# A fused cross-attention and mixture-of-experts kernel: fewer filler matmuls ahead of the first transposes, the low parts of late weights on GpSimd instead of VectorE, and a reordered first unit

## The chip, the cores and the metric

The kernel runs on one core of one Trainium2 chip. The metric is the device time of one execution in microseconds (us), and the time of a kernel is the median of several executions. Before the change the runs gave 1058.31, 1061.67 and 1062.47 us.

## What is computed

For 8 batches of 512 tokens of width 256, in float32, with a context of 512 rows of width 128 for each batch (cut to what matters):

```python
def attention(q, kv):                      # 16 heads of width 64
    qh, kh, vh = split(q @ Wq), split(kv @ Wk), split(kv @ Wv)
    scores = einsum('bhnd,bhmd->bhnm', qh, kh) * 64 ** -0.5
    return join(softmax(scores) @ vh) @ Wo + bo

def experts(x):                            # 8 experts, top 2
    probs = softmax(x @ gate_w.T)
    comb = top-2 of probs, zero elsewhere
    return sum over e of (x @ expert_w[e].T + expert_b[e]) * comb[:, e]

x = x + tanh(g_xattn) * attention(layernorm(x), ctx)
x = x + tanh(g_ffn) * experts(layernorm(x))
```

## The kernel before, in words

Every float32 operand of a matmul is split in two: a high part, which ScalarE (ACT) makes by a copy in the rounded type, and a low part, which is the value minus the high part. Each product is then three matmuls: high by high, high by low, low by high. The low part of what lies in PSUM is made by VectorE (DVE). The low parts of the probabilities (L520) are made by GpSimd (POOL).

A batch is one iteration of 32 **units**: 8 pairs of heads by 4 tiles of 128 tokens. For one unit TensorE (PE) computes the scores of two heads (L1131) into one of two score banks, DVE takes their maximum (L826, `nmax`), ACT makes shifts of it (L655) and the exponential (L664) into one of two slots of `pf`, ACT copies that to half precision (L674, the high part of `p_s`), POOL subtracts (L520, the low part), the queue of SyncE (SP) transposes both parts by DMA, and PE multiplies them with the values six units later (L1147, `PV`). The exponential of unit n waits for the low part of unit n-2, since `pf` has two slots. Between the units each engine does **jobs**: the projections `q`, `k`, `v`, the transposes `xt`, `ot`, `x2t`, the output projection `wo`, the gate and the experts. Jobs are written to three PSUM banks in turn, so job n waits until job n-3 has been read out.

The order of the work is written out by hand: `PE_ORDER`, `ACT_ORDER`, `DVE_ORDER` and `POOL_ORDER` hold one string for each of the 32 rows (units) of an iteration, and each engine works them off in order. The iterations are FIRST (batch 0, without experts), six of LOOP, and LAST; EPI follows. Each iteration also does the experts of the batch before, and the last rows of an iteration do `NEXT_JOBS`, the transposes and first projections of the next batch. For batch 0 these run ahead of it, in the prologue: `xt` 0 and 1, `q` 0, `k` 0, and right behind the first scores `q` 1, `k` 1 and `bound`.

**The prologue.** The inputs and weights are loaded by SP's queue in the order x, context, the first quarter of `wq` (`early`, columns 0 to 255), `wk`, the rest of `wq` (`rest`, 768 columns by two halves of the contraction), `wv`, and small ones. `wq` is staged in `pf`, `wk` and `wv` in the first two slots of `pt_s`, so those must have been read before the first exponential, and before the first and second transposes. ACT makes the high parts (L557 to L592), DVE the low part of `early` (L857) and of `rest` (L871), POOL those of `wk` (L507) and `wv` (L509). PE meanwhile multiplies the identity with itself as a filler (`keep_busy`, L1156; float32, so that each call is two matmuls in the trace): 36 calls ahead of `xt` 0, 5 ahead of `q` 0, 2 ahead of `k` 0. DVE computes the largest `wv` (L865), the largest context value (L734) and their product (L737), which the job `bound` spreads to all partitions, and from which comes `v_mul`, the scale of the values (L770, L799). ACT waits at L595 and L596 for all low parts of `wq` and `wv`, ahead of the first exponential.

**The late weights.** `wo` and the experts' weights come in 12 pieces of 128x512 during FIRST: in the rows of `LATE_AT` (0 to 9, 13, 14) SP issues the load into a stage in `acc` or `xn` (L451), ACT makes the high part three rows later (`LATE_HI`, L650), DVE the low part four rows later (`LATE_LO`, L934). A piece is loaded into a slot of the stage only when that slot's last low part is done (`late_lo`).

```python
if kind == FIRST and n - LATE_LO in LATE_AT:
    h = LATE_AT.index(n - LATE_LO)
    dve.wait_ge(late_hi, h + 1)
    dve.tensor_tensor(late[h][2], late_raw(h), late[h][1].bitcast(F32), ALU.subtract)
```

## Time and profile before

| | before |
|---|---|
| median of 3 runs (range) | 1061.67 us (1058.31 to 1062.47) |
| profiled execution: its own time / span | 1055.02 / 1053.2 us |
| PE busy, matmul | 1007.7 us, 96% of the span |
| DVE busy | 859.2 us, 82% |
| ACT busy | 792.9 us, 75% |
| POOL busy | 610.4 us, 58% |
| DMA, mean | 144 GB/s |
| granted TensorE clock, mean | 0.994 |

The span is the time from the first to the last instruction of the profiled execution. The busy shares are averages over stages with different limits: a few microseconds of prologue, the FIRST iteration, in which PE has no experts to compute, the loop and the end. In the sections below "us" after a row's start is counted from the start of the span, and L numbers are lines of the kernel before.

### The profile page before, as it was taken

The numbers are of one execution on the slowest core, as the hardware profiler recorded it, in microseconds if no ns is written. First come the engines' busy times: TensorE is split into PE (matmuls) and PEld (weight loads), VectorE is DVE, ScalarE is ACT, GpSimd is POOL, SyncE is SP. The second block draws the span as 40 slices with busy tenths as digits, with TensorE's granted clock in tenths as the row PEclk, the third lists the DMA queues.
The fourth block names the chain that finished last, engine by engine and source line by source line (L and its number), as shares of the span: only waits on it lengthen the run. The fifth ranks groups of instructions, "written<-read, shape, count | busy, mean of one in ns | idle before, by whom it ended". The sixth has DMA issues, their size and how long they took to land.

```text
span 1053.2 us, 29369 instructions
## 1 busy us (share of the span) xinstructions
PE 1007.7 (96%) x10752; PEld 779.6 (74%) x10752; DVE 859.2 (82%) x1537; ACT 792.9 (75%) x1404; POOL 610.4 (58%) x359
## 2 busy tenths in 40 slices
PE   7788999999999999999899999999999999999998
PEld 6456777777777777777677787777777787777786
DVE  5898778977888788987689788897889888897737
ACT  4889999767987599866798579885798659975600
POOL 3566767645774467644576446754677446864500
PEclk9999999999999999999999999999999999999999
DMA  4899999977997699965999759977799759996630
GB/s 136 163 207 163 166 175 174 160 112 117 191 184 130 100 169 178 170 120 93 165 179 154 127 89 197 181 135 119 138 184 172 121 101 167 171 156 121 111 62 20
DMA packets 554305, 152.11 MB, mean 144 GB/s; under 512 B 541976, under 2 KB 551600, under 8 KB 554160
## 3 DMA queue, kind: packets, MB, share of 16 engines
q1 hardware_dynamic: 554160, 150.18, 84.0%
q8 instruction: 90, 1.47, 0.6%
q14 instruction: 55, 0.45, 0.2%
HBM read 11.70 MB, written 4.19 MB: 15 GB/s over the span
## 4 chain that ended last, share of the span: by engine, by line
PE 69%; DVE 13%; ACT 7%; issue 7%; DMA 2%; POOL 1%; SPq 0%; DVEq 0%; ACTq 0%; POOLq 0%
PE MB L1021 34%; PE ST L1131 15%; PE PV L1147 13%; DVE nmax L826 4%; PE MB L1033 3%; ACT pf L664 3%; DMA pt_s<-p_s 2%; DVE acc L789 2%; PE ST L1156 2%; ACT p_s L674 1%; POOL p_s L520 1%; DVE m L964 1%; PE MB L1097 1%; DVE ex_s L934 1%; DVE ot_s L815 1%
## 5 line engine op out<-in xcount | busy, mean ns | idle before, releaser
L520 POOL TENSOR_TENSOR p_s<-pf,p_s 128x1024 f16<-128x1024 f32 x256 | 549.7, 2148 | 343.0 <-ACT p_s L674 329.8
L826 DVE TENSOR_REDUCE nmax<-ST 128x2 f32<-128x1024 f32 x256 | 310.9, 1216 | 49.7 <-PE ST L1131 47.4
L664 ACT ACTIVATE pf<-ST,shifts 128x512 f32<-128x512 f32 x512 | 325.4, 693 | 3.9 <-POOL p_s L520 0.4
L674 ACT ACTIVATE p_s<-pf 128x1024 f16<-128x1024 f32 x256 | 272.8, 1066 | 5.6 <-DMA pt_s<-p_s 1.9
L1147 PEld LDWEIGHTS PV<-v_s,pt_s 128*128 128x128 f16 x6144 | 202.9, 98 | 85.1 <-issue 73.4
L1147 PE MATMUL PV<-v_s,pt_s 128*128 128x65 f16 x6144 | 231.6, 194 | 9.8 <-DVE o_n L842 9.3
L1021 PE MATMUL MB<-ex_s,x2t_s 128*128 128x512 f32 x708 | 190.6, 405 | 1.0 <-DVE QL L806 1.0
L789 DVE SCALAR_TENSOR_TENSOR acc<-MB,m,acc 128x256 f32<-128x256 f32 x236 | 113.6, 481 | 45.3 <-PE MB L1021 34.7
L1021 PEld LDWEIGHTS MB<-ex_s,x2t_s 128*128 128x128 f32 x708 | 125.8, 189 | 29.3 <-issue 2.9
L1131 PE MATMUL ST<-KH,QH 64*128 64x512 f32 x512 | 125.6, 487 | 22.8 <-ACT pf L664 17.2
L655 ACT ACTIVATE shifts<-nmax 128x2 f32<-128x2 f32 x256 | 53.5, 212 | 96.6 <-DVE nmax L826 91.1
L1021 PEld LDWEIGHTS MB<-wo_s,ot_s 128*128 128x128 f32 x768 | 99.2, 190 | 11.4 <-DVE ot_s L815 5.1
L1021 PE MATMUL MB<-wo_s,ot_s 128*128 128x256 f32 x768 | 105.0, 286 | 1.6 <-DVE ot_s L815 1.3
L1021 PE MATMUL MB<-xt_s,wq_s 128*128 128x512 f32 x384 | 104.1, 406 | 0.5 <-issue 0.5
L1131 PE MATMUL ST<-KL,QH 64*128 64x512 f32 x512 | 102.0, 393 | 0.0
L1131 PE MATMUL ST<-KH,QL 64*128 64x512 f32 x512 | 101.8, 393 | 0.0
L1131 PEld LDWEIGHTS ST<-KH,QH 64*128 64x128 f32 x512 | 48.2, 184 | 67.7 <-issue 31.7
L574 ACT ACTIVATE ot_s<-MB 128x512 fp32r<-128x512 f32 x64 | 38.6, 605 | 61.0 <-PE MB L1033 61.0
L1021 PEld LDWEIGHTS MB<-xt_s,wq_s 128*128 128x128 f32 x384 | 67.5, 189 | 13.1 <-issue 1.8
L842 DVE SCALAR_TENSOR_TENSOR o_n<-PV,o_mul,rden 128x256 f32<-128x256 f32 x128 | 62.0, 484 | 4.5
L1021 PE MATMUL MB<-wv_s,kv_s 128*128 128x512 f32 x192 | 57.1, 422 | 2.5 <-DVE QL L806 2.5
L818 DVE SCALAR_TENSOR_TENSOR v_s<-MB,v_mul,v_s 128x512 f16<-128x512 f32 x64 | 46.9, 744 | 13.1 <-ACT v_s L578 13.1
(129 smaller groups left out, 1091.2 us busy)
## 6 DMA issues: line engine op xcount, KB each, us to landing
pt_s<-p_s SPq DMA_TRANSPOSE x512, 3.4
xin<-x SPq DMA_DIRECT2D x7, 512.0 KB, 4.6
out<-acc SPq DMA_DIRECT2D x7, 512.0 KB, 3.5
kvin<-kv_t SPq DMA_DIRECT2D x8, 256.0 KB, 4.4
acc<-expert_t SPq DMA_DIRECT2D x6, 256.0 KB, 4.1
pf<-wq SPq DMA_DIRECT2D x1, 768.0 KB, 7.6
xin<-x SPq DMA_DIRECT2D x2, 256.0 KB, 3.0
pt_s<-wk SPq DMA_DIRECT2D x1, 512.0 KB, 6.1
```

The source lines that it names most:

```text
L520: pool.tensor_tensor(p_s[:, slot, 1, :, :], pf[:, u % 2, :, :], p_s[:, slot, 0, :, :], ALU.subtract).then_inc(p_lo, 1)
L574: last = act.activation(ot_s[:, 0, name[1] % GROUP, :], m[:, :], ACT.Copy)
L655: act.activation(shifts[:, u % 2, :], nmax[:, u % 2, :], ACT.Identity, bias=P_SHIFT, scale=SCALE)\
L664: last = act.activation(pf[:, u % 2, i, :], ST[u % 2][:, i, :], ACT.Exp, bias=shifts[:, u % 2, i:i + 1], scale=SCALE)
L674: act.activation(p_s[:, it.ring(p, u, P_SLOTS), 0, :, :], pf[:, u % 2, :, :], ACT.Copy).then_inc(p_hi, 1)
L789: last = dve.scalar_tensor_tensor(acc[:, t, :], m[:, DIM * i:DIM * (i + 1)], comb[:, t, 2 * e + i:2 * e + i + 1], acc[:, t, :], ALU.mult, ...
L818: last = dve.scalar_tensor_tensor(v_s[:, 1, t, g * HH:(g + 1) * HH, 0:HEAD], m[:, :].rearrange("p (h d) -> p h d", d=HEAD), v_mul[:, 0:1], ...
L826: dve.tensor_reduce(nmax[:, t % 2, :], ST[t % 2][:, :, :], AX.X, ALU.max, negate=True)\
L842: dve.scalar_tensor_tensor(dst, outs[:, :, 0:HEAD], o_mul[:, 0:1], rden[:, :].unsqueeze(2).broadcast_to([P, TT, HEAD]), ALU.mult, ALU.mult ...
L1021: last = pe.matmul(dst, s, m, start=(k == 0), stop=(k == n - 1))
L1131: last = pe.matmul(ST[t % 2][:, i, :], queries[r, s, tile(t)], keys[r, s, :], start=(n == 0), stop=(n == len(terms) - 1))
L1147: last = pe.matmul(PV[:, col:col + HEAD + 1], pt_s[:, slot, a, i, k, :], v_s[:, c, k, (2 * p + i) % HEADS, :], start=(k == 0 and n == 0), ...
```

## The change

1. `BUSY_PRO`: the filler calls ahead of the first transposes go from 36 to 15.
2. The low parts of the 12 late weights move from DVE (row n+4) to POOL (row n+3).
3. The low part of `rest` is made in two halves: DVE makes one, behind the job `k` 0 and ahead of the first maximum; POOL makes the other, between `wk` and `wv`. ACT waits for both halves and no longer for `wv`. SP waits for `wv`'s low part ahead of the transposes of unit 1, and PE ahead of `q` 2 for both halves.
4. `NEXT_JOBS`: `bound` comes ahead of `q` 1 and `k` 1. The list sets the order in the prologue; for the other iterations the jobs stand in `PE_ORDER`, which is unchanged. The low part of `eb` and the scaling of `bo_t` on DVE come behind the take of `k` 1.
5. In row 0 of FIRST ACT does the copy of unit 0 ahead of the high part of the first values.

```diff
--- before.py
+++ after.py
@@ -115,7 +115,7 @@
 LATE_AT = list(range(10)) + [13, 14]
 LATE_SLOT = [0, 1, 2, 3, 0, 1, 2, 3, 0, 1, 0, 1]
 LATE_IN_XN = 8
-LATE_HI, LATE_LO = 3, 4
+LATE_HI, LATE_LO = 3, 3
 
 
 def job_of(token):
@@ -127,7 +127,7 @@
 PLACED = [job_of(token) for row in PE_ORDER for token in row.split() if token not in ("scores", "values")]
 
 
-NEXT_JOBS = [("xt", 0), ("xt", 1), ("q", 0), ("k", 0), ("q", 1), ("k", 1), ("bound",)]
+NEXT_JOBS = [("xt", 0), ("xt", 1), ("q", 0), ("k", 0), ("bound",), ("q", 1), ("k", 1)]
 
 LATE_JOBS = [("ot", PAIRS - 2), ("ot", PAIRS - 1)] + [("wo", ROUNDS - 1, j) for j in range(MT)]
 SUMMED = [name for name in PLACED if name[0] in ("bias", "expert")]
@@ -143,7 +143,7 @@
 PRO_JOBS = 4
 NEXT_X2T = [name for name in LAST_JOBS if name[0] == "x2t"][0]
 BUSY_VALUES = 3
-BUSY_PRO = {("xt", 0): 36, ("q", 0): 5, ("k", 0): 2}
+BUSY_PRO = {("xt", 0): 15, ("q", 0): 5, ("k", 0): 2}
 BUSY_EPI = {("ot", PAIRS - 1): 3, ("wo", ROUNDS - 1, 0): 6, NEXT_X2T: 24, ("router",): 5, ("logits",): 3}
 
 JOBS = {PRO: NEXT_JOBS, EPI: LATE_JOBS + LAST_JOBS}
@@ -332,7 +332,7 @@
         wq_in, wq_rest_in, wk_in, wv_in = sem("wq_in"), sem("wq_rest_in"), sem("wk_in"), sem("wv_in")
         small_in = sem("small_in")
         late_in = [sem(f"late_in{n}") for n in range(4)]
-        w_hi, wq_lo, w_lo = sem("w_hi"), sem("wq_lo"), sem("w_lo")
+        w_hi, wq_lo, wq_rest_lo, w_lo = sem("w_hi"), sem("wq_lo"), sem("wq_rest_lo"), sem("w_lo")
         late_hi, late_lo = sem("late_hi"), sem("late_lo")
         const_pool, const_dve = sem("const_pool"), sem("const_dve")
         tanh_done = sem("tanh_done")
@@ -449,6 +449,8 @@
                     if LATE_SLOT[h] in LATE_SLOT[:h]:
                         sp.wait_ge(late_lo, h - LATE_SLOT[:h][::-1].index(LATE_SLOT[h]))
                     sp.dma_start(late_raw(h), late[h][0]).then_inc(late_in[LATE_SLOT[h]], 16)
+                if it.kind == FIRST and n == 1:
+                    sp.wait_ge(w_lo, 2)
                 turn_hi(it, *divmod(n, TT))
                 turn_lo(it, *divmod(n, TT))
                 if n == 9 and it.kind != LAST:
@@ -505,7 +507,9 @@
             pool.wait_ge(ln1_done, 1)
             pool.wait_ge(w_hi, 2)
             pool.tensor_tensor(wk_s[:, 1, :], stage_k, wk_s[:, 0, :].bitcast(F32), ALU.subtract).then_inc(w_lo, 1)
-            pool.wait_ge(w_hi, 3)
+            pool.wait_ge(w_hi, 4)
+            pool.tensor_tensor(wq_s[:, 1, 1, rest], stage_q[:, 1, rest], wq_s[:, 0, 1, rest].bitcast(F32),
+                               ALU.subtract).then_inc(wq_rest_lo, 1)
             pool.tensor_tensor(wv_s[:, 1, :], stage_v, wv_s[:, 0, :].bitcast(F32), ALU.subtract).then_inc(w_lo, 1)
             pool.wait_ge(w_hi, 5)
             pool.tensor_tensor(gt_s[:, 1, :, :], gt_f[:, :, :], gt_s[:, 0, :, :].bitcast(F32), ALU.subtract)\
@@ -547,6 +551,11 @@
                         power(it.b + 2, ln1_var, ln1_rstd, ln1_shift)
                     elif part == "context" and it.kind != LAST:
                         context_low(it)
+                if it.kind == FIRST and n - LATE_LO in LATE_AT:
+                    h = LATE_AT.index(n - LATE_LO)
+                    pool.wait_ge(late_hi, h + 1)
+                    pool.tensor_tensor(late[h][2], late_raw(h), late[h][1].bitcast(F32), ALU.subtract)\
+                        .then_inc(late_lo, 1)
 
             run(pool, row)
             power(BATCHES, ln2_var, ln2_rstd, ln2_shift)
@@ -593,7 +602,7 @@
                     act.activation(tg[:, :], gates[:, :], ACT.Tanh).then_inc(tanh_done, 1)
                 take_hi(pro, name)
             act.wait_ge(wq_lo, 2)
-            act.wait_ge(w_lo, 2)
+            act.wait_ge(wq_rest_lo, 1)
 
             def context_high(it):
                 act.wait_ge(kv_in, 16 * it.b + 32)
@@ -618,7 +627,10 @@
 
             def row(it, n):
                 b, kind = it.b, it.kind
-                for part in ACT_ORDER[n].split():
+                parts = ACT_ORDER[n].split()
+                if kind == FIRST and n == 0:
+                    parts.sort(key=lambda part: part == "hi")
+                for part in parts:
                     at = count.get(part, 0)
                     count[part] = at + 1
                     if part == "hi":
@@ -866,17 +878,17 @@
                        .then_inc(const_dve, 1)
                     dve.wait_ge(const_dve, 1)
                     bound(0)
-                if name == ("q", 1):
+                take(pro, name)
+                if name == ("k", 0):
                     dve.wait_ge(w_hi, 4)
-                    dve.tensor_tensor(wq_s[:, 1, :, rest], stage_q[:, :, rest], wq_s[:, 0, :, rest].bitcast(F32),
+                    dve.tensor_tensor(wq_s[:, 1, 0, rest], stage_q[:, 0, rest], wq_s[:, 0, 0, rest].bitcast(F32),
                                       ALU.subtract).then_inc(wq_lo, 1)
-                if name == ("bound",):
+                if name == ("k", 1):
                     dve.wait_ge(w_hi, 6)
                     dve.tensor_tensor(eb_s[32:32 + EXPERTS, :], eb[32:32 + EXPERTS, :],
                                       eb_s[32:32 + EXPERTS, :].bitcast(F32), ALU.subtract).then_inc(const_dve, 1)
                     dve.wait_ge(tanh_done, 1)
                     dve.tensor_scalar(bo_t[:, :], bo_t[:, :], tg[:, 0:1], None, ALU.mult).then_inc(const_dve, 1)
-                take(pro, name)
 
             for name in JOBS[PRO][:PRO_JOBS]:
                 take_first(name)
@@ -928,11 +940,6 @@
                         moments(ln2_step, b, ln2_var)
                     elif part.startswith("route") and kind != FIRST:
                         route(it, int(part[-1]))
-                if kind == FIRST and n - LATE_LO in LATE_AT:
-                    h = LATE_AT.index(n - LATE_LO)
-                    dve.wait_ge(late_hi, h + 1)
-                    dve.tensor_tensor(late[h][2], late_raw(h), late[h][1].bitcast(F32), ALU.subtract)\
-                       .then_inc(late_lo, 1)
 
             GATE_STEPS = 18
             ROUTE_PARTS = 7
@@ -1053,6 +1060,7 @@
                     pe.wait_ge(kv_lo, it.b + 2)
                 elif kind == "q" and it.kind == FIRST and name[1] == 2:
                     pe.wait_ge(wq_lo, 2)
+                    pe.wait_ge(wq_rest_lo, 1)
                 elif kind == "v" and it.kind == FIRST:
                     pe.wait_ge(w_lo, 2)
                 elif kind == "bound":
```

How DVE's order moves at the end of the prologue. Before, from the context's maximum to the second score maximum:

```order
L734 TENSOR_REDUCE kmax<-kvin 128x1
L737 TENSOR_TENSOR kmax<-kmax,wv_max 128x1
L806 TENSOR_TENSOR QL<-MB,QH 128x512
L806 TENSOR_TENSOR KL<-MB,KH 128x512
L826 TENSOR_REDUCE nmax<-ST 128x2
L871 TENSOR_TENSOR wq_s<-pf,wq_s 128x2x768
L806 TENSOR_TENSOR QL<-MB,QH 128x512
L806 TENSOR_TENSOR KL<-MB,KH 128x512
L875 TENSOR_TENSOR eb_s<-o_n,eb_s 8x256
L878 TENSOR_SCALAR bo_t<-bo_t,tg 128x256
L770 TENSOR_SCALAR v_div<-MB 128x1
L799 RECIPROCAL v_mul<-v_div 128x1
```

The same place on DVE in the changed kernel (its own line numbers):

```order
L746 TENSOR_REDUCE kmax<-kvin 128x1
L749 TENSOR_TENSOR kmax<-kmax,wv_max 128x1
L818 TENSOR_TENSOR QL<-MB,QH 128x512
L818 TENSOR_TENSOR KL<-MB,KH 128x512
L884 TENSOR_TENSOR wq_s<-pf,wq_s 128x768
L838 TENSOR_REDUCE nmax<-ST 128x2
L782 TENSOR_SCALAR v_div<-MB 128x1
L811 RECIPROCAL v_mul<-v_div 128x1
L818 TENSOR_TENSOR QL<-MB,QH 128x512
L818 TENSOR_TENSOR KL<-MB,KH 128x512
L888 TENSOR_TENSOR eb_s<-o_n,eb_s 8x256
L891 TENSOR_SCALAR bo_t<-bo_t,tg 128x256
```

The subtraction for `wq` is half as long and stands ahead of the first maximum, and `v_div` and `v_mul` stand behind it, ahead of `q` 1 and `k` 1.

POOL from the prologue on, before (`p_s` is the low part of a unit's probabilities):

```order
L507 TENSOR_TENSOR wk_s<-pt_s,wk_s 128x1024
L509 TENSOR_TENSOR wv_s<-pt_s,wv_s 128x1024
L511 TENSOR_TENSOR gt_s<-o_n,gt_s 128x16
L520 TENSOR_TENSOR p_s<-pf,p_s 128x1024 x10
L534 TENSOR_TENSOR x<-xin,bo_t 128x1024
```

The same place on POOL in the changed kernel:

```order
L509 TENSOR_TENSOR wk_s<-pt_s,wk_s 128x1024
L511 TENSOR_TENSOR wq_s<-pf,wq_s 128x768
L513 TENSOR_TENSOR wv_s<-pt_s,wv_s 128x1024
L515 TENSOR_TENSOR gt_s<-o_n,gt_s 128x16
L524 TENSOR_TENSOR p_s<-pf,p_s 128x1024 x4
L557 TENSOR_TENSOR wo_s<-acc,wo_s 128x512
L524 TENSOR_TENSOR p_s<-pf,p_s 128x1024
L557 TENSOR_TENSOR wo_s<-acc,wo_s 128x512
L524 TENSOR_TENSOR p_s<-pf,p_s 128x1024
L557 TENSOR_TENSOR wo_s<-xn,wo_s 128x512
```

The half of `wq` stands ahead of `wv`, and from unit 3 on a piece of a late weight stands behind each unit's low part, twelve in all (units 3 to 12, 16 and 17).

## Rows read from the trace of the kernel before

**Rows 1.** Engines' busy time by stretch: times, engines (instructions), clock, DMA share, GB/s

```profile
210.00:330.00 120.00, 119.18 (x1310) 91.93 (x1309) 101.21 (x186) 97.32 (x172) 75.17 (x42) 1.00 0.90 149
...
38.90:94.92 56.02, 44.65 (x535) 32.64 (x534) 49.48 (x67) 48.76 (x90) 36.76 (x20) 0.97 1.08 203
...
94.92:150.00 55.08, 51.45 (x636) 40.07 (x637) 43.59 (x64) 52.30 (x93) 38.55 (x19) 0.97 1.01 161
```

**Rows 2.** The chain of waits from 0 to 45 us: start, us, what

```profile
3.04 9.97 PE ST L1156 x72
...
15.50 1.63 PE MB L1021 x6
...
21.92 1.68 DVE wq_s L871
...
23.86 1.27 ACT pf L664 x2
...
26.48 3.70 PE MB L1021 x9
...
31.26 1.24 DVE nmax L826
```

**Rows 3.** Timeline of the prologue: start, us, engine, instruction [idle before]

```profile
7.19 1.38 DVE L728 TENSOR_SCALAR xn<-xin,mv,rstd 128x256 f32<-128x256 f32 x4
8.90 1.06 ACT L561 ACTIVATE wk_s<-pt_s 128x1024 fp32r<-128x1024 f32 x1 [0.92 <-DMA pt_s<-wk]
...
13.48 1.09 ACT L570 ACTIVATE xt_s<-MB 128x512 fp32r<-128x512 f32 x2 [3.53 <-PE MB L1033]
14.11 1.29 DVE L808 TENSOR_TENSOR xt_s<-MB,xt_s 128x512 fp32r<-128x512 f32 x2 [4.81 <-ACT xt_s L570]
14.46 1.06 ACT L587 ACTIVATE wv_s<-pt_s 128x1024 fp32r<-128x1024 f32 x1
15.59 2.41 POOL L509 TENSOR_TENSOR wv_s<-pt_s,wv_s 128x1024 fp32r<-128x1024 f32 x1 [3.14 <-ACT wv_s L587]
17.28 0.58 ACT L568 ACTIVATE QH<-MB 128x512 fp32r<-128x512 f32 x1
18.94 0.69 DVE L806 TENSOR_TENSOR KL<-MB,KH 128x512 fp32r<-128x512 f32 x1 [0.32 <-ACT KH L568]
...
28.12 0.69 ACT L578 ACTIVATE v_s<-MB,v_mul 128x512 f16<-128x512 f32 x1 [2.02 <-DVE v_mul L799]
```

**Rows 4.** The load of `wv`: its issue in the timeline

```profile
3.73 0.47 SPq L413 DMA_DIRECT2D pt_s<-wv  x1
```

**Rows 5.** The DMA view to 25 us: size, median us from issue to landing

```profile
pt_s<-wv SPq DMA_DIRECT2D x1, 512.0 KB, 8.3
```

**Rows 6.** PE alone by stretches of 1 us: busy (matmuls begun), granted clock, DMA

```profile
6.00:7.00 1.00, 1.00 (x8) 1.00 0.97 366
7.00:8.00 1.00, 1.00 (x11) 1.00 0.99 392
...
27.00:28.00 1.00, 1.00 (x4) 0.52 0.00 0
```

**Rows 7.** Timeline: a low part of probabilities on POOL, a late weight on DVE

```profile
39.11 2.14 POOL L520 TENSOR_TENSOR p_s<-pf,p_s 128x1024 f16<-128x1024 f32 x1 [0.45 <-ACT p_s L674]
...
39.59 2.21 DVE L934 TENSOR_TENSOR wo_s<-acc,wo_s 128x512 fp32r<-128x512 f32 x1 [0.78 <-ACT wo_s L650]
```

**Rows 8.** Line L934: ns min/median/max, first and last start us

```profile
L934 DVE TENSOR_TENSOR ex_s<-acc,ex_s x6: 674/1453/2583, 54.6 to 93.3; 128x512 fp32r<-128x512 f32 x6
...
L934 DVE TENSOR_TENSOR wo_s<-xn,wo_s x2: 1622/1658/1694, 47.9 to 51.2; 128x512 fp32r<-128x512 f32 x2
```

**Rows 9.** Waits from 38.90 to 94.92: us in total, times, longest

```profile
POOL p_s L520 <- ACT p_s L674: 18.7, 12, 2.9
...
ACT shifts L655 <- DVE nmax L826: 7.0, 5, 1.9
```

**Rows 10.** Groups on POOL over the span: count, busy us, mean ns, idle before

```profile
L520 POOL TENSOR_TENSOR p_s<-pf,p_s 128x1024 f16<-128x1024 f32 x256 | 549.7, 2148 | 343.0 <-ACT p_s L674 329.8 <-DMA pt_s<-p_s 11.2
...
L525 POOL TENSOR_TENSOR kv_s<-kvin,kv_s 128x512 fp32r<-128x512 f32 x7 | 9.1, 1297 | 32.7 <-ACT kv_s L601 32.7
```

## The prediction

> **What bounds the kernel now.** I read the busy time by stretch first. In the loop PE is busy 119.18 of 120 us [rows 1]: nothing the change touches runs there, and every batch takes as long as its matmuls. Two stretches are left. Up to about 31 us the chain of waits goes in single file over PE, ACT and DVE. From 38.90 to 94.92 us (units 4 to 18 of FIRST, in which all twelve late weights are split) no engine is full: PE 44.65, DVE 49.48, ACT 48.76, POOL 36.76 of 56.02 us [rows 1]. From there to 150 us ACT is busy 52.30 of 55.08 us [rows 1], the change touches nothing, and the stretch should only move. So what is gained or lost by 95 us is handed on to the end, since PE then only begins its full loop earlier or later.
>
> In the chain of the prologue the reader is to see three long pieces [rows 2]: fillers, 9.97 us; the low part of `wq`, 1.68 us between the first maximum and the first exponential; and nine matmuls of the values, 3.70 us, at the granted clock of about half [rows 6]. The first exponential starts at 23.86, the maximum of unit 2 at 31.26 [rows 2]; at that maximum I measure the prologue's gain.
>
> **The start, step by step.** The fillers run from 3.04 to 13.01. Their rate rises from 8 to 11 a microsecond at 7 us [rows 6]. 30 matmuls instead of 72: 26 are begun by 7 us, by the rows before 7 us and the 8 in the last, and four at the faster rate end at 7.4. The last tile is normalised at 7.19 + 1.38 = 8.57 [rows 3], so the eight transposes now wait for DVE and end near 9.3; the fillers cost nothing any more. ACT is at the high part of `wk` until 8.90 + 1.06 = 9.96, since its load lands late [rows 3]. The high parts of `xt` run from 9.9 to 11.0 where they ran from 13.48, and the low parts end at 11.85 instead of 15.40 [rows 3]. Next in line is the load of `wv`: issued at 3.73 [rows 4] and 8.3 us to landing [rows 5], it is there at 12.0 to 12.5. So ACT starts `wv` at 12.3 and not at 14.46 [rows 3]: of the 3.5 us that the transposes come earlier only 2.2 are left. All that stands between `wv` and the high part of `q` 0 on ACT takes 17.28 - 14.46 = 2.82 us [rows 3] and stays, so that part starts at 15.1. The low part of `k` 0 ended at 19.63 [rows 3] and now ends at 17.0, if `k` 0 follows as closely: **2.6 us** gained at the first scores.
>
> Then the moved subtraction. DVE starts its half of `rest` at 17.0. It reads two tensors from SBUF, and a look at rows 7 shows what that means: at 39.59 a late weight started on DVE while POOL worked from 39.11 to 41.25, and it ended at 41.80, 0.55 us after POOL, though alone it takes 0.67 [rows 8]. POOL has the high parts of `wq` at 14.8 here, does its half in 768/1024 of 2.41 us [rows 3], 1.8 us, and then `wv`, from 16.6 to 19.0. So DVE's half waits and ends near 19.8 (0.55 + 0.27 for the 256 further columns), 1.75 us after the scores are ready. The first maximum follows, and the first exponential at 21.2 instead of 23.86: still 2.6 us. The old 1.68 us behind the maximum are gone, and a wait of about the same size stands ahead of it. From below the cost of this half is 0.9 us alone, hidden behind the first scores, and from above 2.4 us, all of `wv`; I take 1.75, as the order of starts gives it.
>
> Behind it `bound` is taken 0.4 us after the first maximum, so `v_mul` no longer stands behind `q` 1, `k` 1, `eb` and `bo_t`, and ACT's wait of 2.02 us for it [rows 3] is gone. The copy of unit 0 stands ahead of the values and does not need `v_mul` at all. PE can do the first values' job while ACT is at the exponential; the second and third still need the banks of `q` 1 and `k` 1. I work out the low parts of `q` 1 and `k` 1 by 24.3, the maximum of unit 1 at 25.1 to 26.3, the low part of the first values, and the maximum of unit 2 at 27 instead of 31.26: **4.0 us** gained (2.6 kept, 1.4 more as the nine value matmuls are no longer one block behind a wait). `eb` and `bo_t` are only moved and cost what they did. The new wait of SP for `wv` (19.0) costs nothing: the transposes of unit 1 come ten microseconds later. The wait of PE ahead of `q` 2 is long met.
>
> **The late weights.** DVE gets rid of twelve subtractions. Alone one takes 0.674 us, the median of six is 1.453 [rows 8], since most start under POOL; together about 18 us. What this holds up is ACT: it waited 7.0 us for maxima [rows 9]. POOL gets twelve of the shape of its context step, 1.297 us each [rows 10]: 15.6 us. Its waits for ACT were 18.7 us there [rows 9], so there is room, but only just: 36.76 + 15.6 = 52.4 us of work in what were 56.02 [rows 1]. ACT's own work, 48.8 us, allows a gain of 7.2; POOL's allows 3.6, and that only if it never waits. A unit and a late weight take 2.15 + 1.30 = 3.45 us on POOL [rows 10], against some 48.76 / 15 = 3.25 us a unit on ACT. POOL becomes the tightest engine in units 3 to 12. Its bubbles (at the start of the stretch, and where a copy comes late) I put at 1.3 us, a tenth of a microsecond for each piece: **2.3 us** gained. Bounds: 7.0 gained, ACT's waits [rows 9], if POOL's order lets ACT run freely, and 8.6 lost, as the first rival has it; I stay near POOL's own floor of 3.6, since its work is counted from rows and only its bubbles are a guess.
>
> The Trainium skill speaks against this part: "GPSIMD Engine Reference", section Engine selection, puts elementwise work with two inputs on VectorE, since GpSimd is about twice as slow. The rows agree on the size, 1.297 against 0.674. By that rule alone the twelve would cost 12 x 0.62 = 7.5 us and the sum would be 3.5 us slower, near 1065; the median of 1.453 and the free time of POOL are why I go by the rows.
>
> Sum: 4.0 + 2.3 = 6.3 us. The profiled execution took 1055.02 us (span 1053.2 and 1.8 around it) and would come to 1048.7. The median of the runs lies 6.6 us above it, so for the changed kernel's median I forecast 1061.67 - 6.3 = 1055.4 us. About 0.5%, 5.3 us, is what a measurement of this kernel can tell from no change.
>
> **The rivals.**
>
> *POOL becomes the bound and it is slower.* A late weight sits between two low parts. If each delays the next low part, the exponential two units later and the scores behind it, 12 x 1.30 = 15.6 us stand on the path, of which the 7.0 us of ACT's waits come back: 8.6 lost, less 4.0 of the start, 4.6 us slower, 1066.3. It decides where more than 11 of the 15.6 us are not hidden. For it: several of POOL's waits were short (0.45 us at 39.11 [rows 7]). Against: they sum to 18.7 us.
>
> *The clock falls at the start.* PE now idles from 10 to 11.9 and from 15 to 17 us, where fillers kept it busy. Between 24 and 26.5 it idled once before, and the clock was 0.52 afterwards [rows 6]. Six matmuls took 1.63 us at the full clock, nine would take 2.45 and took 3.70 at the half [rows 2]: 0.14 us each. Some 15 on the path: 2 us of the gain go, 1057.4. The Trainium skill, "TensorE: Matmul & The Clock Gate", section PE-mode transpose, adds that transposes do not count as busy for the clock. By it the clock would fall already behind the shorter fillers, with the same price.
>
> *More than forecast.* DVE's half is not held up, because POOL starts `wv` later, and POOL keeps up: 1.75 and some 3 us more, a gain of 11, 1050.7.
>
> *The gain is not handed on.* The stretch after 95 us, where DMA was busy at a share of 1.01 [rows 1], takes back what was gained; near 1061.
>
> **How the numbers follow.** Forecast (a gain of 3 to 9 us) 0.56, more 0.13, clock 0.13, not handed on 0.08, POOL as the bound 0.10. Range: 1050.5 to 1062.0, from the good rival to no gain; it leaves out the slower one and half of what is beyond either end. Faster by over 0.5%: 0.13 and 0.42 of the forecast's 0.56, 0.55. Slower by over 0.5%: 0.06 of the last. Within: 0.39.
>
> **What would show it.** First transposes at about 8.7; ACT's `wv` at 12.3 behind its DMA; DVE's half of `wq` drawn out to about 2.8 us, ending 0.8 behind POOL's `wv`; first exponential at 21, maximum of unit 2 near 27. In the middle stretch ACT's waits for maxima gone, waits for POOL's low parts in their place, and POOL above 90% busy in units 3 to 12. Wrong it is if the unit-2 maximum comes as forecast and the end doesn't, or if POOL's low parts of units 4 to 18 take more than the 56 us they did.

## The result, and the profile after

The changed kernel takes 1050.38 us (median of 5 runs, 1048.92 to 1050.84) against 1059.11 (5 runs, 1056.07 to 1062.47) of the kernel before. The ratio is 0.991, with a 95% interval from 0.989 to 0.9929. That is faster by 8.7 us at the medians. The forecast was 6.3 us: the direction was right, the size too small, and 1050.38 lies just outside the range, whose lower end was 1050.5.

The two profiled executions differ by less: 1055.02 before, 1048.92 after, 6.1 us. The sum had been made against the first of them, so the total of the forecast fits the traces. Its parts don't: one was too large, one too small, and a third (what is given back later) stood at nothing. That they sum to nearly the right number is luck.

The page of the changed kernel, its first lines:

```profile
span 1047.1 us, 29286 instructions
...
PE 1002.5 (96%) x10710; PEld 773.6 (74%) x10710; DVE 846.3 (81%) x1525; ACT 792.6 (76%) x1404; POOL 627.3 (60%) x372
```

PE has 42 matmul instructions fewer (the fillers), DVE lost 13 us of work, and POOL took on 17.

The timeline of the start of the changed kernel (start, us, engine, instruction, idle time before it), answering to [rows 3]:

```profile
3.03 5.22 PE L1164 MATMUL ST<-ident 128*128 128x128 f32 x30 [3.03 <-POOL ident L492]
...
9.47 1.06 ACT L570 ACTIVATE wk_s<-pt_s 128x1024 fp32r<-128x1024 f32 x1 [0.76 <-DMA pt_s<-wk]
...
12.71 1.06 ACT L596 ACTIVATE wv_s<-pt_s 128x1024 fp32r<-128x1024 f32 x1 [1.20 <-DMA pt_s<-wv]
...
15.22 1.80 POOL L511 TENSOR_TENSOR wq_s<-pf,wq_s 128x768 fp32r<-128x768 f32 x1 [2.17 <-ACT wq_s L598]
15.55 0.57 ACT L577 ACTIVATE QH<-MB 128x512 fp32r<-128x512 f32 x1
16.98 2.38 POOL L513 TENSOR_TENSOR wv_s<-pt_s,wv_s 128x1024 fp32r<-128x1024 f32 x1
17.36 2.81 DVE L884 TENSOR_TENSOR wq_s<-pf,wq_s 128x768 fp32r<-128x768 f32 x1
...
24.93 2.33 POOL L524 TENSOR_TENSOR p_s<-pf,p_s 128x1024 f16<-128x1024 f32 x1 [4.68 <-ACT p_s L686]
...
25.29 2.12 DVE L891 TENSOR_SCALAR bo_t<-bo_t,tg 128x256 f32<-128x256 f32 x1
27.33 1.21 DVE L838 TENSOR_REDUCE nmax<-ST 128x2 f32<-128x1024 f32 x1
...
29.12 1.21 DVE L838 TENSOR_REDUCE nmax<-ST 128x2 f32<-128x1024 f32 x1
```

Read it from the top. The fillers end at 8.25, the load of `wv` is what ACT waits for (1.20 us), and its high part of `q` 0 starts at 15.55 instead of 17.28. DVE's half of `wq` (17.36) starts just behind POOL's `wv` (16.98) and takes 2.81 us; it ends at 20.17, 0.8 behind POOL. The surprise is `bo_t`: the scaling of 256 columns takes 2.12 us, where it took 0.35 before. It starts at 25.29, in the middle of POOL's first low part (24.93 to 27.26), and ends 0.15 us behind it. In the kernel before it ran while POOL was idle:

```profile
27.41 0.35 DVE L878 TENSOR_SCALAR bo_t<-bo_t,tg 128x256 f32<-128x256 f32 x1
```

The maximum of unit 1 stands behind it, at 27.33 and not at 25.1 as forecast, and that of unit 2 starts at 29.12: 2.1 us earlier than before [rows 2], not 4.0.

By the maximum of unit 4 (36.11 before, 35.12 after) only 1.0 of the 2.1 are left. PE alone in the changed kernel from 31 to 37 us:

```profile
31.00:37.00 6.00, 4.79 (x17) 0.50 0.47 91
```

The granted clock is at the lower level (1.2 of 2.4 GHz) from 30.3 to 37.2 us. A pair of score matmuls takes 0.80 us there instead of 0.50, and the maxima of units 3 and 4 wait for these matmuls. Before, this place ran at the full clock. The low clock comes with the loss but isn't shown to be all of it: in another execution of the kernel before (e5 below) units 2 to 4 took 6.0 us, as here, at the full clock up to 35.8 us.

The middle, in the stretches of time of [rows 1], and in that from the maximum of unit 5 to that of unit 19; columns as there:

```profile
38.90:94.92 56.02, 47.85 (x597) 34.86 (x596) 39.27 (x64) 53.33 (x97) 52.04 (x33) 1.00 1.09 200
...
94.92:150.00 55.08, 51.38 (x649) 39.45 (x647) 41.81 (x62) 52.79 (x94) 39.82 (x19) 1.00 1.11 172
```

```profile
38.57:87.69 49.12, 41.67 (x503) 30.20 (x503) 32.77 (x54) 46.69 (x86) 46.91 (x30) 1.00 1.09 201
```

DVE went from 49.48 us to 39.27 in the same stretch of time [rows 1], in which it gets further now, and POOL from 36.76 to 52.04. From the maximum of unit 5 to that of unit 19 both ACT (46.69 of 49.12 us) and POOL (46.91, 95%) are full. Two neighbours on POOL there, and the waits from 38.57 to 87.69 us (in total, times, longest):

```profile
52.15 2.15 POOL L524 TENSOR_TENSOR p_s<-pf,p_s 128x1024 f16<-128x1024 f32 x1
54.24 1.29 POOL L557 TENSOR_TENSOR ex_s<-acc,ex_s 128x512 fp32r<-128x512 f32 x1
```

```profile
POOL p_s L524 <- ACT p_s L686: 1.8, 3, 1.2
```

```profile
ACT pf L676 <- POOL p_s L524: 1.0, 1, 1.0
...
ACT shifts L667 <- DVE nmax L838: 0.7, 1, 0.7
```

The late weight takes 1.29 us, as forecast. POOL's waits for ACT fell from 18.7 us [rows 9] to 1.8, ACT's for maxima from 7.0 to 0.7, and ACT waited only once for POOL, 1.0 us. The maximum of unit 19, first before, then after:

```profile
94.85 1.21 DVE L826 TENSOR_REDUCE nmax<-ST 128x2 f32<-128x1024 f32 x1
```

```profile
87.69 1.21 DVE L838 TENSOR_REDUCE nmax<-ST 128x2 f32<-128x1024 f32 x1
```

So 7.2 us are gained at unit 19: 2.1 by unit 2 and 5.0 behind it (1.0 by unit 4 and 6.2 behind it). By the maximum of unit 31 (131.59 before, 125.59 after) 6.0 are left, and these stay to the end.

One execution is a rough measure: two more of the changed kernel (e6 and e15 below) have the maximum of unit 19 at 90.17 and 89.52 and that of unit 31 at 127.30 and 127.44, and a second one of the kernel before has 96.43 and 133.20. A difference of 2 us between single traces can come from this.

### The profile page after: what moved, and what is told of

It is laid out like the page before. It is cut to its first block, busy times and chain, and to the rows that moved or that the text cites. A ratio compares the mean times of both kernels' runs of the same rounds, so it can differ in the third digit from the quotient of the medians.

```text
span 1047.1 us, 29286 instructions
## 1 busy us (share of the span) xinstructions
PE 1002.5 (96%) x10710; PEld 773.6 (74%) x10710; DVE 846.3 (81%) x1525; ACT 792.6 (76%) x1404; POOL 627.3 (60%) x372
## 4 chain that ended last, share of the span: by engine, by line
PE 71%; DVE 10%; issue 6%; ACT 5%; DMA 4%; POOL 3%; SPq 1%; DVEq 0%; ACTq 0%; POOLq 0%
PE MB L1028 34%; PE ST L1139 16%; PE PV L1155 14%; PE MB L1040 3%; DVE nmax L838 3%; POOL p_s L524 2%; DMA pt_s<-p_s 2%; ACT pf L676 2%; DVE acc L801 2%; ACT p_s L686 1%; DMA pt_s<-wv 1%; PE ST L1164 1%; PE MB L1105 1%; DVE m L971 1%; DVE ot_s L827 1%
## 5 line engine op out<-in xcount | busy, mean ns | idle before, releaser
L1139 PE MATMUL ST<-KH,QH 64*128 64x512 f32 x512 | 126.1, 488 | 17.9 <-ACT pf L676 10.9
```

Source lines behind the costliest of these rows:

```text
L1139: last = pe.matmul(ST[t % 2][:, i, :], queries[r, s, tile(t)], keys[r, s, :], start=(n == 0), stop=(n == len(terms) - 1))
```

## The experiments

Three parts are told apart in what follows: **F**, the 15 fillers; **L**, the late weights on POOL; **R**, the rest (halves of `wq`, `bound`, first copy). Every run is compared with runs of the kernel before on the same chip. "Unit n" is the start of unit n's score maximum on DVE, which is a mark that all traces share.

### L alone

```diff
-LATE_HI, LATE_LO = 3, 4
+LATE_HI, LATE_LO = 3, 3
```

with the twelve subtractions moved to POOL as in the change, and nothing else.

> The kernel before with the late weights' low parts on POOL at row n+3, nothing else. Theory A (the late weights give the larger share, since DVE no longer blocks the maxima): 4 to 6 us faster than before, maximum of unit 2 where it was (31.3), maximum of unit 19 at 89 to 91 instead of 94.85. Theory B (the gain comes from the start, POOL being full gives nothing): within 1 us of before.

Measured: 1055.35 us (12 runs) against 1058.49, ratio 0.9972 (0.9957 to 0.9987). Unit 2 at 31.06, unit 19 at 87.96:

```profile
87.96 1.21 DVE L831 TENSOR_REDUCE nmax<-ST 128x2 f32<-128x1024 f32 x1
```

That is 6.9 us earlier than before, more than expected, and within 0.3 us of the first profile of the whole change, though it started the stretch 1.9 us later. Yet only 3.9 are left at unit 31 (127.69) and 3.1 in the medians. Where they went can be seen in PE's timeline of this kernel, and its stretches from 114 us (columns as in [rows 1]):

```profile
114.70 1.00 PE L1147 MATMUL PV<-v_s,pt_s 128*128 128x65 f16 x24 [2.31 <-DMA pt_s<-p_s]
115.64 0.80 PE L1131 MATMUL ST<-KH,QH 64*128 64x512 f32 x2
```

```profile
114.00:118.00 4.00, 3.30 (x36) 2.70 (x36) 1.34 (x3) 1.83 (x3) 3.04 (x2) 0.66 0.97 194
```

PE waits 2.31 us for a transpose, and behind that wait the granted clock is 0.66: a pair of score matmuls takes 0.80 us instead of 0.50, which the units ahead of it took. Theory B fell. Of A the mechanism holds, but 3.1 us at the medians is less than its 4 to 6, and a new limit shows in this trace: the transposes by DMA.

### The change without L

```diff
-LATE_HI, LATE_LO = 3, 3
+LATE_HI, LATE_LO = 3, 4
```

with the twelve subtractions back on DVE.

> The changed kernel with the late weights' low parts back on DVE at row n+4. Theory A: 2 to 3 us faster than before only (the start's 2.1 us), maximum of unit 2 near 29.1, of unit 19 near 92.5. Theory B: 6 to 8 us faster than before, as the changed kernel.

Measured: 1054.54 us (9 runs) against 1058.49, ratio 0.995 (0.9931 to 0.997). Unit 2 at 28.91, unit 19 at 93.19. The traces are as expected (1.7 us gained at unit 19), the median gives 4.0, more than expected.

### F alone

```diff
-BUSY_PRO = {("xt", 0): 36, ("q", 0): 5, ("k", 0): 2}
+BUSY_PRO = {("xt", 0): 15, ("q", 0): 5, ("k", 0): 2}
```

> The kernel before with 15 filler calls instead of 36 ahead of the first transposes. If the chain of the start is only fillers, 3 us faster at the first scores and at the end. Theory C (the later parts of the start, the 1.68 us low part of wq behind the first maximum and v_mul behind q 1 and k 1, stay): first scores 2.2 us earlier (17.5), first exponential 21.7, and some 2 us faster at the end. Rival: the fillers keep the clock up, and with fewer it falls during the first 30 us, gain under 1 us.

Measured: 1053.09 us (6 runs) against 1058.49, ratio 0.9944 (0.9923 to 0.9966), 5.4 us. The first two maxima of note in its timeline:

```profile
18.67 1.23 DVE L826 TENSOR_REDUCE nmax<-ST 128x2 f32<-128x1024 f32 x1 [1.06 <-PE ST L1131]
...
27.83 1.22 DVE L826 TENSOR_REDUCE nmax<-ST 128x2 f32<-128x1024 f32 x1
```

Unit 0 is 2.0 us earlier than before, as expected, and unit 2, at 27.83, is 1.3 us **earlier** than in the changed kernel, with the loads as early as there. So in these traces the fillers alone do more for the start than fillers and reordering together. Of the rival the first half came: the clock fell. PE alone from 19 to 22 us:

```profile
19.00:22.00 3.00, 3.00 (x9) 0.50 0.00 0
```

The second half, a gain under 1 us, did not: unit 2 is 3.4 us earlier than before all the same.

### The change without F

```diff
-BUSY_PRO = {("xt", 0): 15, ("q", 0): 5, ("k", 0): 2}
+BUSY_PRO = {("xt", 0): 36, ("q", 0): 5, ("k", 0): 2}
```

> The changed kernel with the 36 filler calls again. The first scores return to 19.7. Theory C: the rest of the start's reordering is worth little, as DVE's half of wq and the scaling of bo_t are held by POOL; 4 to 6 us faster than before. If fillers carry the whole start's gain: the maximum of unit 2 at 31 and about 2 us slower than the changed kernel. Rival (the reordering carries it): equal to the changed kernel within 1 us.

Measured: 1055.67 us (12 runs) against 1058.49, ratio 0.9976 (0.9958 to 0.9995). Unit 0 at 22.04, unit 2 at 31.07 (31.26 before): the fillers carry the whole gain of the start. Unit 19 is at 88.72 and unit 31 at 128.88, so that 3.4 us are given back between them, as with L alone (3.0), and here too PE waits for a transpose (2.7 us). Beside the change's 0.9919 when it was run again (next) that is 0.6%, or some 6 us, slower, more than expected.

### Both kernels again

> The kernel before, unedited. The forecast's sum, 6.3 us, agrees with the two profiled executions (1055.02 and 1048.92), but the medians differ by 8.7. Theory D (the kernel before varies more from run to run, 1056 to 1062, than the changed one, 1049 to 1051, and the profiled execution was one of its fast ones): the runs of this one spread over 4 us or more. Rival: they lie within 2 us, and the first spread was of the chip.

> The changed kernel, unedited. Theory D: the runs spread over 2 us at most, near 1050. Rival: they spread as those of the kernel before do.

Measured, on one chip: before 1060.69 us (12 runs, 1058.32 to 1066.07), the change 1051.52 (9 runs, 1047.93 to 1058.34), its ratio 0.9919 (0.9891 to 0.9946). The changed kernel spreads over 10 us as well, so theory D fell: it does not vary less. But the profile of this execution of the kernel before (e5) shows one piece that does vary, the fillers:

```profile
3.03 10.88 PE L1156 MATMUL ST<-ident 128*128 128x128 f32 x72 [3.03 <-POOL ident L490]
```

```profile
7.00:8.00 1.00, 1.00 (x7) 1.00 1.03 416
...
9.00:10.00 1.00, 1.00 (x11) 1.00 1.00 388
```

The 72 filler matmuls took 10.88 us here, 9.97 in the profile that I had read [rows 2], and 10.16 and 9.74 in two of the other profiles with 36 calls. In each their rate goes up within a microsecond, but at different times: in the second row (PE alone, from 7 to 8 us) the count is still 7, where it was 11 before [rows 6]. These counts take in every matmul that touches the microsecond. By the starts in the traces one filler begins every 0.22 us or so at first and every 0.112 us later, in all executions: the rate doubles. It does so at 6.6 us in the first profile and at 8.5 us in this one, and just there the trace has its first record of the granted clock (in all profiles between 6.05 and 8.60 us). The 1.00 that the column shows ahead of it stands for no record; the spacing says that TensorE ran at the lower of its two levels. With 36 calls the fillers' end sets when `xt` begins, so the whole start is late by as much; with 15 they ended between 8.1 and 9.3 us in all the profiles, ahead of what ACT waits for.

With 15 calls the clock falls sooner afterwards. It first went to 0.50 at 13.8 to 18.8 us in ten of the twelve profiles with 15 calls and no others added, the change's own in this section (e6) among them, and at about 30 us in the other two, which are the first and the last profile of the change. With 36 calls it first fell at 27.0, 26.6, 20.6 and 35.8 us.

### F and L, without R

```diff
-LATE_HI, LATE_LO = 3, 4
+LATE_HI, LATE_LO = 3, 3
-BUSY_PRO = {("xt", 0): 36, ("q", 0): 5, ("k", 0): 2}
+BUSY_PRO = {("xt", 0): 15, ("q", 0): 5, ("k", 0): 2}
```

with the twelve subtractions on POOL.

> The kernel before with 15 filler calls and the late weights' low parts on POOL, and nothing of the reordered start. If the two parts add up (0.9944 and 0.9972 alone) and the reordering is worth nothing, this one is at 0.9916 of before, as the changed kernel (0.9919). If the reordering pays, it is 2 us or more slower than the changed kernel; maximum of unit 2 at 27.8 as with the fillers alone, against 29.1.

Measured: 1052.47 us (6 runs) against 1059.92, ratio 0.9927 (0.9899 to 0.9954). Unit 2 at 26.97, unit 19 at 87.51, unit 31 at 125.33, against 29.12, 87.69 and 125.59 of the change. R costs 2 us at unit 2 here. Behind it nothing can be told: the other two executions of the change have unit 19 at 90.17 and 89.52, 2 us and more behind this one. The three parts from all six kernels, as ratios to the kernel before, from runs on several chips:

| | without R | with R |
|---|---|---|
| neither | 1 | not run |
| L | 0.9972 | 0.9976 |
| F | 0.9944 | 0.995 |
| F and L | 0.9927 | 0.991, 0.9919, 0.9905 |

F is worth some 0.5% (0.0056 alone, 0.0045 beside L, 0.0057 beside L and R, with 0.9919 for the change), L 0.2% to 0.3% (0.0028 alone, 0.0017 beside F, 0.0031 beside F and R). Alone, each of the two differs from 1 beyond its interval; that L adds to F does not stand out as clearly (0.9944 and 0.9927 have intervals that overlap). R costs 0.0004 beside L and 0.0006 beside F, and gives 0.0008 to 0.0022 beside both: no more than the intervals leave open.

### R mended: the bias steps where DVE waits anyway

```diff
-                if name == ("k", 1):
+                if name == ("bound",):
                     dve.wait_ge(w_hi, 6)
                     dve.tensor_tensor(eb_s[32:32 + EXPERTS, :], eb[32:32 + EXPERTS, :],
...
                     dve.tensor_scalar(bo_t[:, :], bo_t[:, :], tg[:, 0:1], None, ALU.mult).then_inc(const_dve, 1)
```

The block itself is the same; under the new name it runs behind the take of `bound`, ahead of `q` 1.

> The changed kernel with the low part of eb and the scaling of bo_t on DVE directly ahead of the take of bound, while DVE waits for ACT anyway. Theory E (bo_t took 2.12 us instead of 0.35, since POOL's first low part held it): it takes 0.35, the maximum of unit 1 starts at 25.0 instead of 27.3, and the end is 2 us earlier than the changed kernel's. Rival: POOL is full from unit 3 on and takes it back, or PE's values are the next wait, gain under 0.7 us.

Measured: 1050.43 us (6 runs) against 1060.91, ratio 0.9897 (0.9873 to 0.9922). The scaling, and units 1, 2, 14 and 19 on DVE:

```profile
21.65 0.35 DVE L891 TENSOR_SCALAR bo_t<-bo_t,tg 128x256 f32<-128x256 f32 x1
...
24.60 1.22 DVE L838 TENSOR_REDUCE nmax<-ST 128x2 f32<-128x1024 f32 x1
...
27.76 1.23 DVE L838 TENSOR_REDUCE nmax<-ST 128x2 f32<-128x1024 f32 x1 [0.81 <-PE ST L1139]
...
69.77 1.41 DVE L725 BATCH_NORM_STATS2 stats<-xin 128x6 f32<-128x256 f32 x4 [3.08 <-DMA xin<-x]
71.09 0.74 DVE L830 SCALAR_TENSOR_TENSOR v_s<-MB,v_mul,v_s 128x512 f16<-128x512 f32 x1
71.74 1.22 DVE L838 TENSOR_REDUCE nmax<-ST 128x2 f32<-128x1024 f32 x1
...
88.11 1.22 DVE L838 TENSOR_REDUCE nmax<-ST 128x2 f32<-128x1024 f32 x1
```

The scaling of `bo_t` is back at 0.35 us and unit 1 2.7 us earlier: that POOL held it is shown. Over all the profiles it took 2.12 or 2.13 us in the six executions in which it began just behind the start of POOL's first low part, and 0.35 or 0.36 in the other eleven. Some 0.4 of the 2.7 come from the loads, which landed earlier here.

How much of it lasts depends on the execution of the change that it is held against. Against the first one 0.9 are left at unit 14 and nothing at unit 19 (88.11 and 87.69). Against the one on the same chip (e6) it is 2.1 at both:

```profile
90.17 1.22 DVE L838 TENSOR_REDUCE nmax<-ST 128x2 f32<-128x1024 f32 x1
```

What can be seen here is that DVE waits 3.08 us for the load of the next batch's x, and that the maximum of unit 14 stands behind its statistics. At the medians it is 1.1 us ahead of the change (1051.52), between the 2 us of theory E and the 0.7 of the rival, and the intervals overlap.

### R mended: `wv` first on POOL

```diff
+            pool.wait_ge(w_hi, 3)
+            pool.tensor_tensor(wv_s[:, 1, :], stage_v, wv_s[:, 0, :].bitcast(F32), ALU.subtract).then_inc(w_lo, 1)
             pool.wait_ge(w_hi, 4)
             pool.tensor_tensor(wq_s[:, 1, 1, rest], stage_q[:, 1, rest], wq_s[:, 0, 1, rest].bitcast(F32),
                                ALU.subtract).then_inc(wq_rest_lo, 1)
-            pool.tensor_tensor(wv_s[:, 1, :], stage_v, wv_s[:, 0, :].bitcast(F32), ALU.subtract).then_inc(w_lo, 1)
```

> The changed kernel with POOL's low part of wv ahead of its half of wq (wv's high part is ready 1.5 us earlier). POOL then ends wq at about 18.0 and DVE's half of wq ends near 18.8 instead of 20.2: first maximum 1.3 us earlier. Theory E: about 1.3 us faster than the changed kernel. Rival: the scaling of bo_t is held by POOL's first low part for as long as before, relative to it, and nothing reaches the end.

Measured: 1055.14 us (7 runs) against 1060.91, ratio 0.9924 (0.9892 to 0.9956), no faster than the change, and unit 1 at 28.36. The first maximum starts at 19.96 against 20.10, though the loads of this execution landed 0.5 us later. But `bo_t` takes 2.12 us under POOL's first low part again, as the rival had it, and PE runs at the lower clock for 9 us:

```profile
15.00:24.00 9.00, 7.59 (x23) 0.50 0.20 58
```

So it says little by itself. With the bias steps moved as well:

> The changed kernel with the bias steps early on DVE and POOL's wv ahead of its half of wq: maximum of unit 1 at 23.3, of unit 2 at 26.5, 1.3 us earlier than with the bias steps alone. If POOL, which is full in units 3 to 12, and the load of x then take it back, as they did with the bias steps alone (1.36 us earlier at unit 2, 0.4 later at unit 19), the end is within 1 us of the changed kernel's.

Measured: 1044.91 us (6 runs) against 1059.92, ratio 0.9867 (0.9837 to 0.9897). DVE's half of `wq`, and unit 1:

```profile
16.54 1.45 DVE L885 TENSOR_TENSOR wq_s<-pf,wq_s 128x768 fp32r<-128x768 f32 x1
...
22.98 1.21 DVE L839 TENSOR_REDUCE nmax<-ST 128x2 f32<-128x1024 f32 x1
```

The half takes 1.45 us and not 2.81. Unit 2 at 25.83, unit 19 at 86.04, unit 31 at 122.44, 3.1 us ahead of the first profile of the change. Here I had expected nothing at the end, and was wrong in this run.

### The statistics of x a row later

```diff
+                if kind == FIRST and n == 13:
+                    parts.remove("sums1")
+                if kind == FIRST and n == 14:
+                    parts.append("sums1")
```

(with the bias steps early; `parts` is DVE's row)

> The changed kernel with the bias steps early, and the statistics of the next batch's x on DVE in row 14 instead of row 13 of FIRST, so that the maximum of unit 14 does not stand behind the load of x. If that load is what took the early start back, the maximum of unit 14 comes at 70.2 instead of 71.7 and the end 1 to 1.5 us earlier. Rival (the DMA transposes, at a share above 1, are the next wait): unit 14 earlier, unit 19 as before, end within 0.7 us of the bias steps alone.

Measured: 1047.69 us (6 runs) against 1059.92, ratio 0.9886 (0.986 to 0.9912). Unit 14:

```profile
67.60 1.22 DVE L838 TENSOR_REDUCE nmax<-ST 128x2 f32<-128x1024 f32 x1
```

4.1 us earlier than 71.74, of which 1.2 were there at unit 2 already in this execution (26.52 against 27.76) and 1.4 at unit 13 (62.70 against 64.12), so some 2.7 to 2.9 are the edit's at unit 14. Unit 19 is at 86.01 instead of 88.11, which is little more than was there without the edit. The kernel of the next section, which doesn't have the edit, is at 70.21 for unit 14 and yet at 85.69 for unit 19:

```profile
85.69 1.22 DVE L838 TENSOR_REDUCE nmax<-ST 128x2 f32<-128x1024 f32 x1
```

So these traces don't show that the edit reaches unit 19, as its rival said. What takes it back, the transposes by DMA or ACT's own load, was not told apart.

### Eight fillers more in the gap before the first scores

```diff
                 produce(pro, name)
+            keep_busy(8)
```

(behind the first four jobs, with the bias steps early)

> The changed kernel with the bias steps early and 8 filler calls between k 0 and the first scores, where PE idled 2 us. If the clock that fell to 0.50 from 18 to 24 us costs time there, it stays at 1.00, the maximum of unit 1 comes at most 0.3 us earlier, that of unit 2 some 1 us earlier, and the runs spread less. Rival: the clock is hidden behind DVE, nothing changes within 0.5 us.

Measured: 1047.62 us (6 runs) against 1059.92, ratio 0.9906 (0.9873 to 0.994). PE alone from 20 to 22 us, first with the bias steps alone, then with the fillers:

```profile
20.00:22.00 2.00, 2.00 (x6) 0.50 0.00 0
```

```profile
20.00:22.00 2.00, 2.00 (x12) 1.00 0.00 0
```

The clock stays up and twice as many matmuls are counted in the two microseconds. Unit 1 gains 0.4 us and unit 2 1.4 (26.39) on the first of the two, whose clock was low from 17.1 to 24.0 us. In the execution of the last section, with the same start, it was low only from 17.9 to 21.3, and that one is no more than 0.1 us behind at units 1 and 2 (24.32 and 26.52). The lower clock in this place is real where it occurs (the changed kernel's first profile had 1.00 there), and this execution, with fillers in the idle time, got past it; in the ratio to before nothing can be told from no change (0.9906 against 0.9897).

### The three mends together, beside the change

The bias steps early, `wv` first, and the statistics a row later; then the first two once more; then the change unedited, all on one chip.

> The changed kernel with the bias steps early, POOL's wv first, and the statistics in row 14. At unit 14 the two earlier edits gave 69.7 and 67.6; if they add, 65.7 here, and the end 1 us or more ahead of the better of the two. If the stretch behind unit 14 (DMA at a share above 1) sets the pace, unit 19 stays near 86 and the end is that of the other two: 1045 to 1047.

> The bias steps early and wv first once more, beside the changed kernel on one chip. If it is faster than the changed kernel, as the calls apart say (0.9867 against 0.9919 of before), 4 to 6 us. If that was the chip or the load times of these runs, 2 us, what the unit-31 maximum moved (122.4 against 125.6 to 127.3).

> The changed kernel, unedited, as the measure for the other two: 0.991 to 0.992 of before.

Measured against 1058.55 us of before: all three 1045.36 (4 runs), ratio 0.9876 (0.9861 to 0.9892); the first two 1047.13 (6 runs), 0.9896 (0.9876 to 0.9917); the change 1047.62 (5 runs), 0.9905 (0.9889 to 0.9921). Unit 14 of all three is at 67.30, not at 65.7, and the first two alone, without the statistics moved, are at 67.86: the parts don't add there. Unit 19 is at 84.98 (84.57 for the first two), unit 31 at 122.36. Two of my expectations fell: the change was better this time than in its two other measurements, and the first two mends are only 0.5 us ahead of it at the medians, though their trace is 5.6 us ahead at unit 31 (121.86 against 127.44). The version with all three is the fastest of the three here, 2.3 us ahead of the change at the medians, with intervals that just touch; the interval of the first two overlaps both.

## Why the prediction was right or wrong

**The direction and the total.** The sum of 6.3 us was made against one profiled execution, and the two profiled executions differ by 6.1. Of the 5.0 us between the forecast of 1055.4 and the measured 1050.38, 2.6 lie in the starting median (1061.67 against 1059.11) and 2.4 in the gain (6.3 against 8.7). The measured medians differ by 8.7, 9.4 and 10.9 us (0.991, 0.9919, 0.9905). The range ended at a gain of 11.2 from the 1061.67 of the three runs I had; the kernel before measured 1059.11, 1058.49, 1060.91, 1059.92 and 1058.55 since. The range took in the unknown costs but not that the starting number was itself uncertain by 2 us.

**"4.0 us gained" at unit 2: wrong.** The trace shows 2.1. Up to the first exponential the steps hold: fillers off the path, the load of `wv` next in line, 1.75 us kept on ACT (`wv` at 12.71 instead of 14.46, where I had put 2.2), DVE's half of `wq` held by POOL's `wv` until 20.2 (forecast 19.8), first exponential at 21.67 (forecast 21.2, with all loads about 0.5 us later). One reading in it was wrong without a cost: 26 fillers were to have begun by 7 us and the last to end at 7.4. The rows count a matmul in every column that it touches; 20 had begun in the trace of the kernel before, and the 15 calls ended at 8.25. What failed is the sentence "`eb` and `bo_t` are only moved and cost what they did". I had seen that two SBUF inputs on DVE wait for POOL, and took a product with one SBUF tensor as free of it; there it took 2.12 instead of 0.35 us, in the one place where the change had put it under POOL's first low part. These 1.8 us, and 0.4 by which the first exponential came later than forecast, about account for the difference between 4.0 and 2.1. Moving it back out gave 2.7 us at unit 1. Of the 2.1, another 1.1 were gone by unit 4, where the clock was at 0.50.

**"2.3 us gained" by the late weights: wrong, too small.** The trace has 5.0 between units 2 and 19. That POOL would be the tightest engine was right: it ran at 95% from unit 5 to 19. The step that failed is its floor of 52.4 us. It has 15 low parts and all 12 late weights in a stretch that ends at the maximum of unit 19. In the trace POOL had done 14 low parts (units 3 to 16) and 11 late weights by then; the low part of unit 17 begins at 88.02 and the twelfth late weight at 90.11, behind the maximum at 87.69, which did not have to wait for them. That is 3.4 us of work too much in the floor, so it was not 3.6 us but some 7 that could be gained. POOL's work from unit 5 to 19 was 46.91 us. The 1.3 us of bubbles were no error to speak of: POOL was idle for 2.2 us of the 49.12. Of the 7.2 us at unit 19 the changed kernel gives back 1.2 by unit 31, where PE waits three times for a transpose (2.6 us in all, at a clock of 1.00), and L alone 3.0 of its 6.9, where PE waits for one and its clock falls: the rival "the gain is not handed on" was right for a part, for which the sum had no term.

**The fillers: the term was mis-sized.** 2.6 us were credited to them at the first scores (2.2 in the trace of the change: 17.50 against 19.68). The part alone gives 5.4 us at the medians (interval 3.6 to 8.2), its trace 2.0 to 2.9 at unit 0 and 1.7 to 3.4 at unit 31, against the two profiles of the kernel before. The 9.97 us in [rows 2] were one value of a piece that came out between 9.74 and 10.88. That accounts for up to 1 us more. The rest of the difference between traces and medians, some 2 us, stays open: the loop differs between executions of one kernel by as much.

**The rivals.** POOL as the bound with a loss did not come: ACT waited once for it. The rival of the clock was right in its mechanism: the clock fell earlier than before in ten of twelve profiles with 15 calls, and in the first profile of the change it was at 0.50 from 30.3 to 37.2 us. Its price of 2 us is not shown: F gained 5.4 us at the medians in spite of it, and where the clock was kept up unit 2 came 1.4 us earlier against one execution and 0.1 against another. Right behind the shorter fillers, as the rule on transposes that the forecast took from the Trainium skill would have it, it fell in none: they had ended by 9.3 us, and the earliest falls were at 13.8 and 14.3, in the two profiles whose `wk` landed last. The Trainium skill's rule in "GPSIMD Engine Reference", section Engine selection, that two-input elementwise work belongs on VectorE, would have left the twelve where they were. The step is indeed twice as long on GpSimd, 1.29 against 0.67, and moving it made the kernel faster (ratio 0.9972 alone), since GpSimd had the time, and on DVE it stood behind GpSimd's own steps: it took 1.63 us there at the median of all twelve, 1.453 at that of the six [rows 8] names.

**R.** That the changed order of the first unit is worth something was forecast (1.4 us) and did not come out: it cost 0.0004 and 0.0006 of the ratio beside L or F alone and gave 0.0008 to 0.0022 beside both, none of it beyond the intervals. R was never run alone. With its one blocked step moved and `wv` taken first it did better in the traces (unit 31 at 122.44 and 121.86, against 125.59 to 127.44 of the change) and in one of the two measurements (0.9867, where the change had 0.9919 and 0.9905); in the other it had 0.9896, which can't be told from the change beside it.

## What to carry to other kernels

Two engines that lock each other out are one resource: when a step on one lands under a long step of the other, its price is the other's remaining time, so look at what runs beside the new place, even for steps that are "only moved". An engine at twice the cost for a step can be the right one if it has the time and the step blocks the one that others wait for. And a filler loop ahead of the first real work costs what the clock lets it cost: shorten it to where the next wait is a load, and then look where the clock falls behind it. When a floor is counted for an engine, count only the work that the mark at the end of the stretch waits for.

## What the runs showed of the hardware that was not expected

A DVE product of one SBUF tensor with a scalar of each partition (float32, 128x256) took 2.12 and 2.13 us under a GpSimd subtraction and 0.35 us without, so it was held as products with two SBUF inputs are. The Trainium skill, "SBUF — State Buffer", section Who interferes with whom, says that one side blocks the other fully, for VectorE's two-port modes and for two SBUF inputs; it counts `tensor_scalar` among the forms that can enter the first. The trace agrees on the full wait (the product ended 0.15 us after GpSimd).

The filler matmuls began every 0.22 us and then every 0.112 us, from 6.05 to 8.60 us on in the seventeen profiles, while the granted clock in the profile's view reads 1.00 before and after. The trace has no clock record ahead of that moment, so a 1.00 at the very start of a program is not a measured one.
